# Memory layer of a transformer kernel: both recalls contract a pair of heads over a block-diagonal copy of the memory

## The reference

```python
def step(carry, inp):                       # scanned over the 32 segments
    mem, z = carry                          # mem: b h 64 64, z: b h 64
    q_s, k_s, v_s, qn_s, kn_s = inp
    scores = jnp.einsum('bhnd,bhmd->bhnm', q_s, k_s) * SCALE
    scores = jnp.where(mask, scores, -jnp.inf)
    sdpa = jnp.einsum('bhnm,bhmd->bhnd', jax.nn.softmax(scores, axis=-1), v_s)
    sq = elu1(qn_s)
    num = jnp.einsum('bhnk,bhkv->bhnv', sq, mem)
    den = jnp.einsum('bhnk,bhk->bhn', sq, z)[..., None]
    out = beta * num / (den + 1e-06) + (1.0 - beta) * sdpa
    sk = elu1(kn_s)
    prev_v = jnp.einsum('bhnk,bhkv->bhnv', sk, mem) / jnp.einsum('bhnk,bhk->bhn', sk, z)[..., None]
    mem = mem + jnp.einsum('bhnk,bhnv->bhkv', sk, v_s - prev_v)
    z = z + sk.sum(axis=2)
    return ((mem, z), out)
```

## Time and profile before

| What | us |
|---|---|
| median of 3 runs | 2560.41 |
| lowest and highest of them | 2554.07, 2563.69 |
| span of the profiled execution | 2623.8 |
| of it the memory layer's setup, about 1729 to 1763 | 34 |
| of it its slots, first to last `recall` | 1763.2 to 2437.9 |
| span over median | 1.025 |

### The profile page before, as it was taken

How to read it: one execution, slowest core, us unless ns; L and a number is a source line. 1 busy time by engine, 2 the same in 40 slices (tenths; PEclk the granted TensorE clock), 3 DMA queues, 4 the chain that set the end, 5 groups by cost and what they waited for, 6 DMA issues and landing times. The chain is left out here.

```text
span 2623.8 us, 79243 instructions
## 1 busy us (share of the span) xinstructions
PE 2176.9 (83%) x30448; PEld 1549.2 (59%) x30448; DVE 1700.0 (65%) x5819; ACT 1437.8 (55%) x3704; POOL 1106.7 (42%) x1076
## 2 busy tenths in 40 slices
PE   6499948589964889899999977948999999999696
PEld 3288845379862233333334336937778777787396
DVE  6722247642336778787878833358999989899522
ACT  5455544355552256455455555537777767776353
POOL 2066644146654120120200004547777777776164
PEclk7699979789986799998989888969999999999798
DMA  4011120011125121111111000121111111111013
GB/s 133 33 42 43 43 85 2 33 32 44 43 93 163 55 58 31 38 39 31 35 46 35 5 33 29 41 85 54 54 53 56 52 53 55 52 56 52 35 42 92
DMA packets 76025, 134.96 MB, mean 51 GB/s; under 512 B 17225, under 2 KB 32264, under 8 KB 73224
## 3 DMA queue, kind: packets, MB, share of 16 engines
q1 hardware_dynamic: 62080, 102.07, 12.6%
q0 software_dynamic: 13568, 27.81, 3.7%
q10 hardware_dynamic: 8, 0.00, 0.0%
HBM read 65.19 MB, written 32.79 MB: 37 GB/s over the span
## 5 line engine op out<-in xcount | busy, mean ns | idle before, releaser
L1544 ACT ACTIVATE ca_pt<-ca_ps 128x512 f32<-128x512 f32 (+3 forms) x768 | 341.1, 491 | 322.3 <-PE ca_ps L1649 137.2
L734 PE MATMUL ffn_ps<-ffn_xst,ffn_up_w 128*128 128x128 f32 x3392 | 420.8, 278 | 0.2 <-issue 0.2
L734 PEld LDWEIGHTS ffn_ps<-ffn_xst,ffn_up_w 128*128 128x128 f32 x3392 | 402.9, 195 | 1.2 <-issue 1.2
L857 DVE TENSOR_TENSOR ffn_hid<-ffn_sg,ffn_ps 128x512 f32<-128x512 f32 x212 | 145.8, 688 | 359.2 <-PE ffn_ps L734 110.9
L576 POOL DMA_INDIRECT ffn_xs<-ffn_x,ffn_token_at x212 | 205.2, 968 | 301.5 <-DVE ffn_token_at L840 165.5
L581 POOL DMA_INDIRECT ffn_y<-ffn_ys,ffn_result_at x212 | 208.8, 985 | 139.2 <-DVE ffn_ys L863 82.3
L1645 PE MATMUL ca_ps<-ca_stacks 75*128 75x512 bf16 (+3 forms) x768 | 245.2, 342 | 18.3 <-ACT ca_pt L1544 10.7
L1777 DVE TENSOR_REDUCE ca_m_far<-ca_ps 128x1 f32<-128x128 f32 (+5 forms) x384 | 236.7, 616 | 30.3 <-PE ca_ps L1623 27.9
L643 ACT ACTIVATE ffn_sg<-ffn_ps 128x512 f32<-128x512 f32 x212 | 125.7, 593 | 233.6 <-remote 182.3
L1623 PE MATMUL ca_ps<-ca_stacks 72*128 72x512 bf16 (+3 forms) x768 | 223.4, 356 | 34.1 <-DVE ca_m_near L1778 21.9
L1778 DVE CUSTOM_DVE_ANT_0 ca_spill<-ca_ps,ca_bias_q 128x256 f32<-128x256 f32 (+1 forms) x512 | 201.1, 397 | 10.9 <-PE ca_ps L1623 10.9
(11 more groups left out here) (340 smaller groups left out, 4742.0 us busy)
## 6 DMA issues: line engine op xcount, KB each, us to landing
im_mates<-im_t SPq DMA_DIRECT2D x256, 128.0 KB
ffn_got<-ffn_y SPq DMA_DIRECT2D x48, 256.0 KB, 5.8
ca_stacks<-scratch_q_piece SPq DMA_DIRECT2D x16, 576.0 KB
ca_stacks<-scratch_k_piece SPq DMA_DIRECT2D x48, 192.0 KB
ffn_x<-ffn_xn SPq DMA_DIRECT2D x32, 256.0 KB, 2.0
w_w<-in_L_ffn_experts_w_dram SPq DMA_DIRECT2D x2, 2048.0 KB, 12.0
ffn_xs<-ffn_x,ffn_token_at POOLq DMA_INDIRECT x212
ffn_y<-ffn_ys,ffn_result_at POOLq DMA_INDIRECT x212
```

The lines of the kernel that those rows point to most:

```text
L734: last = nc.tensor.matmul(ps[:, bank, j * P:j * P + P], up_w[:, n % WS, first + j * P:first + j * P + P], xst[:, n % 2, :], start=True, st ...
L1544: nc.scalar.activation(pt[:, i % 8, lo - c0:hi - c0], ps[:, tile_bank(i), lo - c0:hi - c0], ACT.Exp, scale=SCALE).then_inc(p_ready, 1)
```

## The change

`prev` and `num` become 8 matmuls each instead of 16 (`for_pairs`: 2 blocks x 4 batches). Each contracts all 128 partitions, both heads of a pair, against 130 moving columns. The moving operand is a new tile, `mem_by`, in which the memory of the even head stands on partitions 0 to 63 in the first 65 columns and that of the odd head on 64 to 127 in the last 65, with zeros in the other two blocks. POOL sets the zeros once, and the starting value 1.0e-6 of column 65. After each `remember(j)`, SP copies the two halves of `mem` into their blocks with two DMAs (64 partitions x 520 values each), behind the two `mates` DMAs of the same turn, and the next `prev` of that group of heads waits for them (`placed`). `prev` now fills bank 0 and `num` bank 1, with the four heads in their natural order, so the views that DVE reads are rearranged, and `learn` picks `uu` by the new order; the counts of DVE's instructions and their sizes stay.

```diff
-        PR, NU, SC = 0, PB * E1, 2 * PB * E1
+        SC = 2 * PB * E1
+        mem_by = s.sb("mem_by", [P, NQ, 2, BATCH, PB, E1])
...
-        prev_view, num_view = (both_banks(c, PB * E1).rearrange("p e (k d) -> p e k d", k=PB) for c in (PR, NU))
+        prev_view, num_view = (ps[:, bank, 0:QH * E1].rearrange("p (h d) -> p h d", d=E1) for bank in range(2))
...
                     for odd in range(2):
                         sp.dma_start(mates[1 - odd:P:2, k % 2, :], t2[odd:P:2, k % 2, :]).then_inc(mates_ready[k % 2], 16)
+                    if 0 <= k - 4 < N - NQ:
+                        j = k - 4
+                        sp.wait_ge(S["mem_ready"], j + 1)
+                        for e in range(2):
+                            half = slice(D * e, D * e + D)
+                            sp.dma_start(mem_by[half, j % NQ, e], mem[half, j % NQ]).then_inc(placed[j % NQ], 16)
...
                 pool.wait_ge(S["made"], 13)
+                nc.gpsimd.memset(mem_by[:], 0.0).then_inc(S["made"], 1)
+                pool.wait_ge(S["made"], 14)
+                for e in range(2):
+                    nc.gpsimd.memset(mem_by[D * e:D * e + D, :, e, :, :, D:E1], 1.0e-6).then_inc(S["made"], 1)
+                pool.wait_ge(S["made"], 16)
...
+                def for_pairs(fn):
+
+                    for blk in range(PB):
+                        for b in range(BATCH):
+                            last = fn(blk, b, slice(SEG * b, SEG * b + SEG))
+                    return last
...
                 def prev(j):
                     q, r = j % NQ, j % 3
                     if j >= NQ:
-                        pe.wait_ge(S["mem_ready"], j - NQ + 1)
-                    for_heads(lambda half, bank, blk, b, tok: nc.tensor.matmul(ps[tok, bank, PR + blk * E1:PR + blk * E1 + E1], el[half, r, PB + blk, tok], mem[half, q, b, blk, :],
-                                                                               start=True, stop=True, skip_group_check=True))
+                        pe.wait_ge(placed[q], 32 * (j // NQ))
+                    for_pairs(lambda blk, b, tok: nc.tensor.matmul(ps[tok, 0, blk * 2 * E1:blk * 2 * E1 + 2 * E1], el[:, r, PB + blk, tok], mem_by[:, q, :, b, blk, :],
+                                                                   start=True, stop=True, skip_group_check=True))
...
-                    for_heads(lambda half, bank, blk, b, tok: nc.tensor.matmul(ps[tok, bank, NU + blk * E1:NU + blk * E1 + E1], el[half, r, blk, tok], mem[half, q, b, blk, :],
-                                                                               start=True, stop=True, skip_group_check=True)).then_inc(S["recalled"], 1)
+                    for_pairs(lambda blk, b, tok: nc.tensor.matmul(ps[tok, 1, blk * 2 * E1:blk * 2 * E1 + 2 * E1], el[:, r, blk, tok], mem_by[:, q, :, b, blk, :],
+                                                                   start=True, stop=True, skip_group_check=True)).then_inc(S["recalled"], 1)
...
-                pe.wait_ge(S["made"], 13)
+                pe.wait_ge(S["made"], 16)
...
-                    nc.vector.tensor_tensor(sorted_heads(m1[:, r]), num_view[:, :, :, 0:D], over(dn[:], D), ALU.mult).then_inc(S["m1_ready"], 1)
+                    nc.vector.tensor_tensor(m1[:, r], num_view[:, :, 0:D], bl(dn[:], D), ALU.mult).then_inc(S["m1_ready"], 1)
```

More of the change, by code:

```diff
@@ L1900, in memory_layer @@
                  "u_ready", "den_ready", "dn_ready", "m1_ready", "p_ready", "share_ready", "own_gated", "rsum_ready", "pn_ready", "pt_ready", "pte_ready",
-                 "upd_ready", "mem_ready", "weighed", "ot_copied", "out_ready", "x_ready", "stats")
+                 "upd_ready", "mem_ready", "placed_a", "placed_b", "placed_c", "placed_d", "weighed", "ot_copied", "out_ready", "x_ready", "stats")
         S = {n: s.sem(n) for n in names}
         mates_ready = (S["mates_even"], S["mates_odd"])
+        placed = (S["placed_a"], S["placed_b"], S["placed_c"], S["placed_d"])
         def both_banks(first, width):
@@ L2167, in learn @@
                                 tok = slice(SEG * b, SEG * b + SEG)
-                                last = nc.tensor.matmul(b_up[half, b, blk * E1:blk * E1 + E1], keys[tok, blk, half], uu[tok, r, PB * parity + blk, :],
+                                last = nc.tensor.matmul(b_up[half, b, blk * E1:blk * E1 + E1], keys[tok, blk, half], uu[tok, r, 2 * blk + parity, :],
                                                         start=True, stop=True, skip_group_check=True)
@@ L2217, in _ @@
                 dve.wait_ge(S["g_ready"], 1)
-                dve.wait_ge(S["made"], 13)
+                dve.wait_ge(S["made"], 16)
                 nc.vector.tensor_scalar_add(gate[:, 1:3, :], gate[:, 1:3, :], 1.0).then_inc(S["setup"], 1)
@@ L2260, in recall @@
                                                    ALU.mult, ALU.add).then_inc(S["s1_ready"], 1)
-                    nc.vector.reciprocal(rd[:].rearrange("p (e k) -> p e k", e=2), prev_view[:, :, :, D]).then_inc(S["rd_ready"], 1)
+                    nc.vector.reciprocal(rd[:], prev_view[:, :, D]).then_inc(S["rd_ready"], 1)
                     dve.wait_ge(S["s1_ready"], j + 1)
@@ L2264, in recall @@
                     dve.wait_ge(S["rd_ready"], j + 1)
-                    nc.vector.scalar_tensor_tensor(dn[:].rearrange("p (e k) -> p e k", e=2), num_view[:, :, :, D], 1.0e-6,
-                                                   gate[:, 1, q * QH:q * QH + QH].rearrange("p (k e) -> p e k", e=2), ALU.add, ALU.mult).then_inc(S["den_ready"], 1)
+                    nc.vector.scalar_tensor_tensor(dn[:], num_view[:, :, D], 1.0e-6, gate[:, 1, q * QH:q * QH + QH], ALU.add, ALU.mult).then_inc(S["den_ready"], 1)
                     dve.wait_ge(S["lifted"], j + 1)
@@ L2270, in recall @@
                     for h in range(QH):
-                        e, n = h // PB, h % PB
-                        last = nc.vector.scalar_tensor_tensor(uu[:, r, h, 0:D], prev_view[:, e, n, 0:D], rd[:, h:h + 1], values_of(j)[:, 2 * n + e, :], ALU.mult, ALU.subtract)
+                        last = nc.vector.scalar_tensor_tensor(uu[:, r, h, 0:D], prev_view[:, h, 0:D], rd[:, h:h + 1], values_of(j)[:, h, :], ALU.mult, ALU.subtract)
                     last.then_inc(S["u_ready"], 1)
```

## The result

The changed kernel takes 2581.24 us (median; 2576.34 to 2583.95), the kernel before 2559.61 us in the runs beside it: a ratio of 1.0085, with an interval of 1.006 to 1.0109. That is 21.6 us more, where 33.5 had been forecast. The time lies in the forecast range, the direction is as forecast, and the size is two thirds of it.

A forecast was written before the change was run, and what follows sets the result against it. The bound was taken to be a ring of PE's arc, holding `prev` and `num`, and DVE's `recall`. Slots +29.5 us (23.5 and 6) and setup +4 made 33.5, on 2560.4 giving 2594 us, range 2570 to 2618.

The forecast's parts named there:

- that are late anyway: 61 of 128 slots where DVE came late itself: most of the longer arc hidden, 0.1 us each, +6 us.
- time on an engine spare: PE's `lift_keys`, `project` and `learn`, under DVE's arc in a slot: 0.58 us to spare.
- ring of two engines: Memory layer's slot: PE's arc 2.85 us, DVE's 1.99, two handovers, 5.12 in all; PE's arc grows by 0.35.

The follow-up runs named there:

- e8: e3 with PE's order turned: `prev` put ahead of `lift_values`, `score` moved behind `weigh`, right before `num`; ratio to the kernel before 0.9974.
- e3: The changed kernel with zeroing off the path: the first transposes start before `mem_by` is zeroed, only the first `prev` waits for it; ratio to the kernel before 1.0082.
- e1: The kernel before with the two copies a slot added and waited for by `prev`, but not read, and nothing zeroed; ratio to the kernel before 1.0038.
- e4: The changed kernel with one-column matmuls of constants before `learn`'s own, giving PE its 64 instructions a slot back; ratio to the kernel before 1.0236.

## What to carry to other kernels

Merging two half-height matmuls over a block-diagonal operand halves the instructions and doubles the columns; where the halves already ran side by side, it costs time on the engine, here 0.19 us and 0.06 us a group. Its gain here was indirect and smaller, by fewer instruction packets. Before sizing a term in slots "that are late anyway", sort them by what makes them late: each kind can grow, hide or shrink. Before calling time on an engine spare, look at more than one slot: the slot read here was one of the few without `product`. When a ring of two engines sets the pace, look first for a group in it that could be done ahead of it: moving `prev` out gained 26 us (e8 against e3), more than the two forms of the recall differ by.

## Hardware findings that were not expected

- PE can starve for instructions. With the longer stream (64 more PE instructions a slot than after) and twice the data packets, PE stood still for 8.5 us (e1) and 8.8 us (e4) within `prev`; with either of the two alone for 1.8 us or less. All 40 such stops over 0.25 us in seven traces end 1.20 to 1.73 us after a 16 KB instruction packet landed.
- Where an instruction packet starts within 2 us after the end of `sines`, the `mates` land late: over 2.5 us in 57 of 58 slots of before and in 31 of 31 of after, where undisturbed ones take 2.3 us.
- DVE starts 0.340 us after the start of the last matmul record that it waits for, with 65 columns and with 130. From the recorded end it is 0.125 and 0.067 us.
- A DVE instruction with two inputs in SBUF that overlaps one of POOL ends 0.146 to 0.153 us after POOL's (35 cases). Beside a POOL memset of 3.57 us, eight DVE instructions took 4.09 us instead of 2.14.
- Packets of 2080 bytes took 0.152 us, those of 2048 bytes 0.087 us (medians).
